# Block attention: the second head's scores are shifted inside ScalarE's exponential, the first head's stay with VectorE

## The chip, the cores and the metric

The kernel runs on one core of a Trainium2 chip. A core has five engines that work side by side and meet through semaphores: TensorE (PE in the rows; its weight loads are PEld), VectorE (DVE), ScalarE (ACT), GpSimd (POOL) and SyncE (SP), which issues transfers. The metric is device time in microseconds (us) of one execution, lower is better. A profiled execution gives the trace from which the rows below are taken.

## The reference

128 sequences of 128 tokens go through two layers of width 64. The change touches the first half of one block, a causal attention with 4 query heads and 2 key heads of width 16, whose core is:

```python
h = _rmsnorm(x, ln1_w)
q, k, v = ...                       # per head, q and k with rotary tables
scores = jnp.einsum('bhtd,bhsd->bhts', q, k) / jnp.sqrt(jnp.float32(HD))
scores = jnp.where(causal[None, None], scores, jnp.float32(-1e+30))
att = jax.nn.softmax(scores, axis=-1)
y = jnp.einsum('bhts,bhsd->bhtd', att, v).transpose(0, 2, 1, 3).reshape(Bx, Tx, Cx)
x = x + y @ wo.T
```

The softmax subtracts each row's maximum before the exponential. Everything before (embedding and a first attention) and after (experts, a decay attention, a selected MLP) is left as it was.

## The kernel before

The program is five phases, one after the other, with a barrier between them. The block attention (`phase_block_attention`) is the second. It holds 32 groups of 4 sequences (`GB` = 4; a sequence of 128 tokens is one block of 128 columns), and each group is done in two rounds K, since a round handles two of the four heads: `NQ` = 64 rounds. In round K, `m = K // 2` is the group and `j = K % 2` says which pair of heads. Here a round with j = 0 is called even, one with j = 1 odd. `e` = 0 is the first head of the pair and `e` = 1 the second.

One round goes like this. TensorE writes the scores of both heads to `bS` (`b_S` in the rows), two PSUM banks, one for each head, 512 columns each: two products that lay down the causal mask (L643), and eight small ones with the scores (L650). VectorE takes the maximum over each block of 128 columns (L924, 8 maxima for each row: 2 heads, 4 blocks), then subtracts it from both heads in one instruction that moves 1024 columns from PSUM to `pr` in SBUF (L930). ScalarE exponentiates `pr` in place in one instruction (L840). In the next round TensorE transposes `pr` head by head into `bT` (`turn`, L662), ScalarE copies each result out (`keep`, L785), and TensorE multiplies it with the values (L672).

There is one `bS`. So the scores of round K + 1 may be written once those of round K have been read, and `scores` waits for that on the semaphore `shifted`. There are two `pr`.

Each engine runs a list written out by hand for K = -7 to 72, in which the steps of several groups are interleaved (projections for later groups, output and routing of earlier ones), and each engine works its list strictly in order. On ScalarE the exponential of round K stands behind both `keep` of round K - 1, and in even rounds also behind `logits` (L807); behind it stand the small root computations of the layer norms (L847 to L857 in even rounds, L863 to L870 in odd ones). On VectorE the maximum and the shift stand next to each other in every round. GpSimd and SyncE take no part in the scores; GpSimd uses what ScalarE's small steps make (`b_rms` for `b_xn` at L603, `b_ss` for `moe_rows` at L615).

Of the kernel before, what the change touches and what calls it, by code (L numbers as in the profile page):

```python
# [6 lines left out]
ALU = mybir.AluOpType  # L7
ACT = mybir.ActivationFunctionType
# [5 lines left out]
P = 128  # L14
D = 64
GB = 4
# [50 lines left out]
def over(ap, width):  # L67

    return ap[:, :, None].to_broadcast([ap.shape[0], ap.shape[1], width])
# [415 lines left out]
def phase_block_attention(nc, dram, H, rows, logits, sent, ident, NB):  # L485
# [8 lines left out]
    with ExitStack() as ctx:  # L494
        m_ = Mem(nc, ctx)
# [19 lines left out]
        k1 = m_.sb("b_k1", [P, W])  # L515
        v = [m_.sb(f"b_v{u}", [P, GB, NKV, STRIP]) for u in range(2)]
        mx = [m_.sb(f"b_mx{u}", [P, 2, GB]) for u in range(2)]
        pr = [m_.sb(f"b_pr{u}", [P, 2, W]) for u in range(2)]
        pT = [m_.sb(f"b_pT{u}", [P, W]) for u in range(PT)]
        attT = m_.sb("b_attT", [P, W])  # L520
# [6 lines left out]
        bS = m_.ps("b_S", [P, 2, 512])  # L527
# [4 lines left out]
        kept = m_.sem("b_kept")  # L532

        U = {name: m_.sem(f"b_{name}") for name in
             ("scored", "max_made", "shifted", "exped", "turned", "pT_kept")}

        G = {name: m_.sem(f"bg_{name}") for name in
             ("summed", "mean_made", "centred", "squared", "spread", "log_var", "rstd_made", "x_made", "rstd_sq",
# [11 lines left out]
        def after(eng, name, n):  # L550

            if n >= 0:
                eng.wait_ge(G[name], min(n, NG - 1) + 1)

        def cols(b):
            return slice(b * P, (b + 1) * P)

        def place(b):

            return b % 2, slice(b // 2 * P, (b // 2 + 1) * P)  # L560
# [9 lines left out]
        with nc.Block() as block:  # L570
# [60 lines left out]
            def _(pe):  # L631
                pe.wait_ge(ready, READY)

                def scores(K):
                    m, j = K // 2, K % 2
                    s = m % 2
                    if j == 0:
                        pe.wait_ge(G["q_kept"], m + 1)
                        pe.wait_ge(G["k_made"], m + 1)
                    if K >= 1:  # L640
                        pe.wait_ge(U["shifted"], K)
                    for e in range(2):
                        nc.tensor.matmul(bS[:, e, :], ident_b[:], hide[:, None, :].to_broadcast([P, GB, P]),  # L643
                                         start=True, stop=False)
                    for b in range(GB):
                        half, c = place(b)
                        c = slice(half * HALF + c.start, half * HALF + c.stop)
                        for e in range(2):
                            r = slice(STRIP * (2 * j + e), STRIP * (2 * j + e + 1))
                            last = nc.tensor.matmul(bS[:, e, cols(b)], q[s][r, c], k0[s][r, c], start=False,  # L650
                                                    stop=(b == GB - 1))
                    last.then_inc(U["scored"], 1)

                def turn(K, e):
                    w = 2 * K + e
                    pe.wait_ge(U["exped"], K + 1)
                    if w >= 1:
                        pe.wait_ge(U["pT_kept"], w)
                    if K % 2 and e == 0:
                        after(pe, "y_made", K // 2 - 1)  # L660
                    for b in range(GB):
                        last = nc.tensor.transpose(bT[:, cols(b)], pr[K % 2][:, e, cols(b)], ident[:])  # L662
                    last.then_inc(U["turned"], 1)
# [112 lines left out]
            def _(act):  # L776
# [3 lines left out]
                def keep(K, e):  # L780
                    w = 2 * K + e
                    act.wait_ge(U["turned"], w + 1)
                    if w >= PT:
                        act.wait_ge(G["attended"], (w - PT) // NH + 1)
                    nc.scalar.activation(pT[w % PT][:], bT[:], ACT.Copy).then_inc(U["pT_kept"], 1)  # L785

                for K in range(FIRST, LAST + 1):
# [22 lines left out]
                    else:  # L810
# [25 lines left out]
                        if 0 <= K - 1 < NQ:  # L836
                            keep(K - 1, 1)
                    if 0 <= K < NQ:
                        act.wait_ge(U["shifted"], K + 1)
                        nc.scalar.activation(pr[K % 2][:], pr[K % 2][:], ACT.Exp).then_inc(U["exped"], 1)  # L840
                    if j == 0:
                        n = m + 3
                        if there(n):
# [29 lines left out]
            def _(dve):  # L873
# [21 lines left out]
                for K in range(FIRST, LAST + 1):  # L895
# [25 lines left out]
                    if 0 <= K < NQ:  # L921
                        u = K % 2
                        dve.wait_ge(U["scored"], K + 1)
                        nc.vector.tensor_reduce(mx[u][:].rearrange("p e b -> p (e b)"),  # L924
                                                bS[:].rearrange("p e (b t) -> p (e b) t", t=P), AX, ALU.max)\
                            .then_inc(U["max_made"], 1)
                        dve.wait_ge(U["max_made"], K + 1)
                        if K >= 2:
                            dve.wait_ge(U["turned"], 2 * (K - 1))
                        nc.vector.tensor_tensor(pr[u][:].rearrange("p e (b t) -> p (e b) t", t=P),  # L930
                                                bS[:].rearrange("p e (b t) -> p (e b) t", t=P),
                                                over(mx[u][:].rearrange("p e b -> p (e b)"), P), ALU.subtract)\
                            .then_inc(U["shifted"], 1)
                    if j == 0:
                        n = m + 3
                        if there(n):
# [1457 lines left out]
```

## Time and profile before

| | us |
|---|---|
| median of 3 runs | 2656.37 |
| the 3 runs | 2630.66, 2656.37, 2674.85 |
| the profiled execution | 2635.22 |
| its span, first to last instruction | 2633.4 |
| block attention: first scores to the last shift | 357.5 to 727.6 |
| maxima on VectorE in it (L924) | 64 of 1.22 each |
| shifts on VectorE in it (L930) | 64 of 1.22 each |
| exponentials on ScalarE in it (L840) | 64 of 1.05 each |

A row of the timeline says when an instruction (or a run of like ones) began, counted from the start of the span, how long it took, engine, line, operation, result and operands with their shapes; in brackets stands how long the engine had been idle and what ended that. The duration of a run of matmuls reaches to the modelled end of the last, so it overlaps the next row a little.

### The profile page before, as it was taken

The page shows a single profiled execution, that of the slowest core. Times are in us where ns is not written, and L with a number is a line of the kernel's source. Part 1 is how long each engine was busy: PE and PEld are TensorE (multiplying, and loading weights), DVE is VectorE, ACT ScalarE, POOL GpSimd, SP SyncE. Part 2 cuts the span into 40 slices and gives each one's busy share as a digit, 9 for nine tenths or more (in the row PEclk, how much of TensorE's full clock was granted, in tenths as well). Part 3 has the DMA queues.
Part 4 walks back from the last instruction along what each step waited for, and adds up shares of the span by engine and source line. Part 5 has one row for each costly group of instructions (what it writes and reads, how often), then busy time and mean ns, then how long its engine had stood idle before and what let it go on. Part 6 is the DMA issues. An engine that isn't in the chain of part 4 may idle for free. (4 is left out here: it accounts for less than half of the span.)

```text
span 2633.4 us, 56014 instructions
## 1 busy us (share of the span) xinstructions
PE 2170.0 (82%) x20636; PEld 1641.2 (62%) x20636; DVE 1790.5 (68%) x3688; ACT 1297.2 (49%) x2690; POOL 1733.5 (66%) x1900
## 2 busy tenths in 40 slices
PE   6999769999923699997289899889999998998495
PEld 5888647777723445444167677677777776776374
DVE  4899457777759644444377878878888788875524
ACT  1344136666621244443056666666666666664332
POOL 6565024444312577775499999999999999875361
PEclk9999579999955699999587888877778888875577
DMA  2111000000004255567100000000000000000003
GB/s 47 35 41 33 0 9 26 22 26 26 22 20 2 59 133 132 134 131 107 31 6 6 6 5 6 5 5 6 5 6 6 5 5 4 2 2 2 3 1 64
DMA packets 105741, 78.14 MB, mean 30 GB/s; under 512 B 71533, under 2 KB 92269, under 8 KB 105488
## 3 DMA queue, kind: packets, MB, share of 16 engines
q0 software_dynamic: 23344, 53.01, 9.5%
q1 hardware_dynamic: 82144, 21.74, 4.4%
q8 instruction: 161, 2.64, 0.4%
q14 instruction: 92, 0.75, 0.1%
HBM read 56.03 MB, written 18.68 MB: 28 GB/s over the span
## 5 line engine op out<-in xcount | busy, mean ns | idle before, releaser
L1906 DVE TENSOR_TENSOR_SCAN d_later<-d_cont,d_ex 128x768 f32<-128x768 f32 x128 | 279.2, 2182 | 30.8 <-ACT d_ex L1719 30.6
L1689 ACT ACTIVATE d_pT<-d_T 128x384 f32<-128x384 f32 x256 | 125.1, 489 | 291.9 <-PE d_T L1550 291.7
L1550 PE MATMUL d_T<-ident,d_p 128*128 128x128 f32 x768 | 170.7, 341 | 88.8 <-POOL d_p L1475 83.2
L1457 POOL TENSOR_TENSOR d_decay<-d_later,d_posg 128x768 f32<-128x768 f32 x128 | 233.0, 1820 | 7.7 <-DVE d_later L1906 7.7
L1461 POOL TENSOR_TENSOR d_decay<-d_decay,d_rtot 128x512 f32<-128x512 f32 x128 | 183.2, 1431 | 18.4
L1468 POOL DMA_INDIRECT d_moe<-back_rows,slot x128 | 137.6, 1075 | 73.3 <-DVE d_mean L1857 49.9
L1537 PEld LDWEIGHTS d_S<-d_kT,d_qT 16*128 16x128 f32 x2048 | 150.8, 221 | 51.2 <-issue 51.2
L1883 DVE SCALAR_TENSOR_TENSOR d_p<-d_decay,d_R 128x768 f32<-128x768 f32 x128 | 121.6, 950 | 87.5 <-PE d_R L1537 51.9
L1537 PEld LDWEIGHTS d_R<-d_kT,d_qT 16*128 16x128 f32 x2048 | 148.7, 218 | 51.3 <-issue 51.3
L1474 POOL TENSOR_TENSOR d_p<-d_p,d_mx 128x512 f32<-128x512 f32 x128 | 159.2, 1244 | 28.6 <-DVE d_mx L1889 26.8
L1537 PE MATMUL d_S<-d_kT,d_qT 16*128 16x128 f32 (+1 forms) x2048 | 170.0, 314 | 0.0
L1550 PEld LDWEIGHTS d_T<-ident,d_p 128*128 128x128 f32 x768 | 96.0, 165 | 116.9 <-POOL d_p L1475 93.5
L1537 PE MATMUL d_R<-d_kT,d_qT 16*128 16x128 f32 (+1 forms) x2048 | 167.8, 311 | 0.0
L1725 ACT ACTIVATE d_decay<-d_decay 128x768 f32<-128x768 f32 x128 | 107.3, 838 | 79.7 <-POOL d_decay L1462 79.5
L223 POOL DMA_INDIRECT rows<-in_table,idx x128 | 122.0, 953 | 35.6 <-issue 31.3
L1462 POOL TENSOR_TENSOR d_decay<-d_decay,d_rtot 128x256 f32<-128x256 f32 x128 | 140.3, 1096 | 0.0
L1327 DVE TENSOR_TENSOR e_cont<-e_h,e_upto 128x512 f32<-128x512 f32 x91 | 62.9, 691 | 104.7 <-ACT e_upto L1200 104.7
L1608 PE MATMUL d_X<-d_conv,d_xT 128*128 128x128 f32 x640 | 112.7, 354 | 1.5 <-ACT d_xT L1778 1.5
L1608 PEld LDWEIGHTS d_X<-d_conv,d_xT 128*128 128x128 f32 x640 | 111.2, 271 | 2.6 <-ACT d_xT L1778 2.6
L1719 ACT ACTIVATE d_ex<-d_ex 128x768 f32<-128x768 f32 x128 | 107.6, 840 | 7.9 <-DVE d_ex L1875 7.2
L594 POOL TENSOR_SCALAR b_mean<-b_mean 128x4 f32<-128x4 f32 x32 | 7.0, 220 | 156.4 <-DVE b_mean L965 156.3
L1727 ACT ACTIVATE d_decay<-d_decay 128x768 f32<-128x768 f32 x128 | 107.9, 843 | 4.1
(403 smaller groups left out, 6226.1 us busy)
## 6 DMA issues: line engine op xcount, KB each, us to landing
sent_rows<-moe_rows SPq DMA_DIRECT2D x32, 256.0 KB, 2.8
back_rows<-e_ys SPq DMA_DIRECT2D x91, 64.0 KB
out_h<-g_Y SPq DMA_DIRECT2D x8, 512.0 KB, 4.0
rows<-in_table,idx POOLq DMA_INDIRECT x128
d_moe<-back_rows,slot POOLq DMA_INDIRECT x128, 2.5
e_tie<-sent_rows,e_token POOLq DMA_INDIRECT x62
e_pick<-sent_rows,e_token POOLq DMA_INDIRECT x60
e_both<-sent_rows,e_token POOLq DMA_INDIRECT x60, 3.1
```

Of the source, the lines that this page charges most:

```text
L223: pool.indirect_dma_start(rows[u][:, b, :], None, dram["table"], bass.IndirectOffsetOnAxis(ap=idx[u][:, b:b + 1], axis=0))\
L1457: pool.tensor_tensor(decay[d][:], later[u][:, 0:2 * SEG].rearrange("p (e s) -> p e s", e=2), posg[:, h:h + 2, :], ALU.mult).then_inc(U["pl ...
L1461: pool.tensor_tensor(long(decay[d]), long(decay[d]), wide(rtot[u], 1, P), ALU.mult)
L1462: pool.tensor_tensor(short(decay[d]), short(decay[d]), wide(rtot[u], 0, HALF), ALU.mult)\
L1468: pool.indirect_dma_start(moe[n % KEEP_M][:, j, :], None, back_rows, bass.IndirectOffsetOnAxis(ap=slot[:, b:b + 1], axis=0))\
L1474: pool.tensor_tensor(long(p2[w]), long(p2[w]), wide(mx2[u], 1, P), ALU.subtract)
L1537: last = nc.tensor.matmul(bank[:, e, cols], qT[s][r, c, (2 * g + S) * P:(2 * g + S + 1) * P], kT[s][r, c, keys], start=False, stop=(g == 1 ...
L1550: last = nc.tensor.transpose(bT[:, t * P:(t + 1) * P], p2[K % KEEP_P][:, e, t * P:(t + 1) * P], ident[:])
L1608: last = nc.tensor.matmul(X1[:, g * P:(g + 1) * P], xT[:, g, tap:tap + P], conv[:, tap, :], start=(tap == 0), stop=(tap == TAPS - 1))
L1689: nc.scalar.activation(pT[w % KEEP_T][:], bT[:, 0:SEG], ACT.Exp).then_inc(U["pT_kept"], 1)
L1883: nc.vector.scalar_tensor_tensor(p2[w][:], decay[d][:], 1e-5, bR[:, :, 0:SEG], ALU.max, ALU.mult).then_inc(U["weighed"], 1)
L1906: nc.vector.tensor_tensor_scan(later[u][:, 1:1 + 2 * SEG], cont[:], ex[u][:].rearrange("p e s -> p (e s)"), 0.0, ALU.mult, ALU.add)\
```

## The change

The first head keeps its path: VectorE subtracts its maxima (512 columns now) and ScalarE exponentiates them in SBUF in one instruction. The second head no longer passes VectorE: VectorE makes the negative of its four maxima (`minus`, 128x4), and ScalarE reads its scores straight from PSUM, in four instructions of 128 columns, one for each block, with the block's column of `minus` as the bias of the exponential. ScalarE does the second head first. `exped` now counts these four for each round, and the first head has a semaphore of its own, `near_exped`. TensorE's `scores` waits for `exped` as well, since ScalarE now reads `bS`.

```diff
+        minus = [m_.sb(f"b_minus{u}", [P, GB]) for u in range(2)]
...
                     if K >= 1:
                         pe.wait_ge(U["shifted"], K)
+                        pe.wait_ge(U["exped"], GB * K)
...
                 def turn(K, e):
                     w = 2 * K + e
-                    pe.wait_ge(U["exped"], K + 1)
+                    if e == 0:
+                        pe.wait_ge(U["near_exped"], K + 1)
+                    else:
+                        pe.wait_ge(U["exped"], GB * (K + 1))
...
                     if 0 <= K < NQ:
+                        u = K % 2
+                        act.wait_ge(U["minus_made"], K + 1)
+                        if K >= 2:
+                            act.wait_ge(U["turned"], 2 * (K - 1))
+                        for b in range(GB):
+                            nc.scalar.activation(pr[u][:, 1, cols(b)], bS[:, 1, cols(b)], ACT.Exp, bias=minus[u][:, b:b + 1])\
+                                .then_inc(U["exped"], 1)
                         act.wait_ge(U["shifted"], K + 1)
-                        nc.scalar.activation(pr[K % 2][:], pr[K % 2][:], ACT.Exp).then_inc(U["exped"], 1)
+                        nc.scalar.activation(pr[u][:, 0, :], pr[u][:, 0, :], ACT.Exp).then_inc(U["near_exped"], 1)
...
-                        nc.vector.tensor_tensor(pr[u][:].rearrange("p e (b t) -> p (e b) t", t=P),
-                                                bS[:].rearrange("p e (b t) -> p (e b) t", t=P),
-                                                over(mx[u][:].rearrange("p e b -> p (e b)"), P), ALU.subtract)\
-                            .then_inc(U["shifted"], 1)
+                            dve.wait_ge(U["exped"], GB * (K - 1))
+                        nc.vector.tensor_scalar(minus[u][:], mx[u][:, 1, :], -1.0, None, ALU.mult).then_inc(U["minus_made"], 1)
+                        nc.vector.tensor_tensor(pr[u][:, 0, :].rearrange("p (b t) -> p b t", t=P),
+                                                bS[:, 0, :].rearrange("p (b t) -> p b t", t=P),
+                                                over(mx[u][:, 0, :], P), ALU.subtract).then_inc(U["shifted"], 1)
```

ScalarE's list at the end of an even round, and the start of the odd one, in the kernel before (in brackets the semaphores that an instruction waits for):

```order
L785 ACTIVATE b_pT<-b_T 128x512 [waits bg_attended,b_turned]
L807 ACTIVATE logits<-b_XB 128x2x2x8 [waits bg_routed]
L840 ACTIVATE b_pr<-b_pr 128x1024 [waits b_shifted]
L847 ACTIVATE b_rstd<-b_ss 128x4 [waits bg_msq_made,bg_x_made,bg_spread]
L850 ACTIVATE b_rstd<-b_rstd 128x4 [waits bg_log_var]
```

The same place in the changed kernel:

```order
L790 ACTIVATE b_pT<-b_T 128x512 [waits bg_attended,b_turned]
L812 ACTIVATE logits<-b_XB 128x2x2x8 [waits bg_routed]
L849 ACTIVATE b_pr<-b_S,b_minus 128x128 [waits b_turned,b_minus_made]
L849 ACTIVATE b_pr<-b_S,b_minus 128x128 x3
L852 ACTIVATE b_pr<-b_pr 128x512 [waits b_shifted]
L859 ACTIVATE b_rstd<-b_ss 128x4 [waits bg_msq_made,bg_x_made,bg_spread]
```

One instruction on `pr` has become five, and the first four read `bS`; their place behind the copy and the logits is the same.

TensorE's list from the projections of an even round to the scores of the odd one, in the kernel before:

```order
L680 MATMUL b_XA<-b_xT,f_wk 128x256 [waits bg_v_kept,bg_x2_made,bg_xT_kept]
L680 MATMUL b_XB<-b_xT,f_wkp 128x256 [waits bg_logits_kept,bg_yT_kept,bg_q_kept]
L643 MATMUL b_S<-hide,ident_b 128x512 [waits b_shifted]
L643 MATMUL b_S<-hide,ident_b 128x512
L650 MATMUL b_S<-b_k,b_q 128x128 x8
```

The same place in the changed kernel:

```order
L685 MATMUL b_XA<-b_xT,f_wk 128x256 [waits bg_v_kept,bg_x2_made,bg_xT_kept]
L685 MATMUL b_XB<-b_xT,f_wkp 128x256 [waits bg_logits_kept,bg_yT_kept,bg_q_kept]
L645 MATMUL b_S<-hide,ident_b 128x512 [waits b_exped,b_shifted]
L645 MATMUL b_S<-hide,ident_b 128x512
L652 MATMUL b_S<-b_k,b_q 128x128 x8
```

Nothing moved on TensorE; the first product of the scores waits for ScalarE's four instructions as well.

## Rows read from the trace of the kernel before

**Rows 1.** Busy time (count) of the engines by stretch, granted clock, DMA share, GB/s

```profile
400.00:500.00 100.00, 94.96 (x1112) 72.05 (x1108) 75.84 (x130) 66.87 (x171) 42.65 (x68) 1.00 0.08 23
...
720.00:730.00 10.00, 8.37 (x108) 6.32 (x104) 6.16 (x9) 6.36 (x13) 1.91 (x3) 1.00 0.09 28
```

**Rows 2.** Timeline of TensorE, from the scores of one even round to the next

```profile
507.32 0.59 PE L643 MATMUL b_S<-hide,ident_b 128*128 128x512 bf16 x2
...
508.93 0.66 PE L662 MATMUL b_T<-ident,b_pr 128*128 128x128 f32 x4
...
510.37 0.63 PE L662 MATMUL b_T<-ident,b_pr 128*128 128x128 f32 x4 [0.56 <-ACT b_pT L785]
...
511.93 0.70 PE L680 MATMUL b_XB<-b_xT,f_wkp 64*128 64x256 f32 x4
512.56 0.61 PE L643 MATMUL b_S<-hide,ident_b 128*128 128x512 bf16 x2
...
515.91 0.60 PE L747 MATMUL b_XB<-ident,moe_rows 128*128 128x128 f32 x4
...
519.11 0.59 PE L643 MATMUL b_S<-hide,ident_b 128*128 128x512 bf16 x2
```

**Rows 3.** Timeline of ScalarE, the same stretch

```profile
505.91 0.60 ACT L785 ACTIVATE b_pT<-b_T 128x512 f32<-128x512 f32 x1 [0.30 <-PE b_T L662]
506.40 1.05 ACT L840 ACTIVATE b_pr<-b_pr 128x1024 f32<-128x1024 f32 x1
...
507.94 0.20 ACT L870 ACTIVATE b_rms<-b_rms 128x4 f32<-128x4 f32 x1
...
509.63 0.60 ACT L785 ACTIVATE b_pT<-b_T 128x512 f32<-128x512 f32 x1 [0.21 <-PE b_T L662]
...
511.03 0.60 ACT L785 ACTIVATE b_pT<-b_T 128x512 f32<-128x512 f32 x1 [0.54 <-PE b_T L662]
511.59 0.20 ACT L807 ACTIVATE logits<-b_XB 128x32 f32<-128x32 f32 x1
511.68 1.05 ACT L840 ACTIVATE b_pr<-b_pr 128x1024 f32<-128x1024 f32 x1
```

**Rows 4.** Timeline of VectorE, the same stretch

```profile
507.28 0.15 DVE L957 TENSOR_TENSOR b_rsq<-b_rstd 128x4 f32<-128x4 f32 x1
...
510.35 1.22 DVE L930 TENSOR_TENSOR b_pr<-b_S,b_mx 128x1024 f32<-128x1024 f32 x1
```

**Rows 5.** ScalarE instructions by line and shape: busy us, mean ns, idle before

```profile
L1689 ACT ACTIVATE d_pT<-d_T 128x384 f32<-128x384 f32 x256 | 125.1, 489 | 291.9 <-PE d_T L1550 291.7
...
L1189 ACT ACTIVATE e_xT<-e_X,e_ln 128x256 f32<-128x256 f32 x91 | 43.1, 473 | 46.6 <-PE e_X L1119 46.3
L2141 ACT ACTIVATE g_hid<-g_H,g_b 128x512 f32<-128x512 f32 x64 | 40.5, 683 | 33.3 <-PE g_H L2067 33.3
...
L820 ACT ACTIVATE b_xT<-b_XA 128x256 f32<-128x256 f32 x32 | 12.1, 379 | 2.2 <-PE b_XA L694 2.1
...
L832 ACT ACTIVATE b_v<-b_XA 128x128 f32<-128x128 f32 x32 | 8.9, 277 | 1.7 <-PE b_XA L688 1.6
```

**Rows 6.** Timeline of ScalarE in the last phase, two like instructions together

```profile
2499.80 1.26 ACT L2141 ACTIVATE g_hid<-g_H,g_b 128x512 f32<-128x512 f32 x2 [1.64 <-PE g_H L2067]
```

**Rows 7.** Timeline of ScalarE and TensorE at the start of rounds 2 and 63

```profile
368.03 1.05 ACT L840 ACTIVATE b_pr<-b_pr 128x1024 f32<-128x1024 f32 x1
...
368.06 0.61 PE L643 MATMUL b_S<-hide,ident_b 128*128 128x512 bf16 x2
...
723.40 0.60 PE L643 MATMUL b_S<-hide,ident_b 128*128 128x512 bf16 x2
723.49 1.05 ACT L840 ACTIVATE b_pr<-b_pr 128x1024 f32<-128x1024 f32 x1
```

**Rows 8.** Timeline of GpSimd, the same stretch as in groups 2 to 4

```profile
508.92 0.61 POOL L603 TENSOR_TENSOR b_xn<-b_x,b_rms 128x256 f32<-128x256 f32 x1
...
513.47 1.19 POOL L615 TENSOR_TENSOR moe_rows<-b_x,b_ss 128x256 f32<-128x256 f32 x2 [3.25 <-ACT b_ss L857]
```

More of the change, by code:

```diff
@@ L534, in phase_block_attention @@
         U = {name: m_.sem(f"b_{name}") for name in
-             ("scored", "max_made", "shifted", "exped", "turned", "pT_kept")}
+             ("scored", "max_made", "minus_made", "shifted", "near_exped", "exped", "turned", "pT_kept")}
         G = {name: m_.sem(f"bg_{name}") for name in
```

## The prediction

> **What bounds the kernel now.** I began with the busy time by stretch. In the stretch from 400 to 500 us, in the middle of the block attention, TensorE is busy 94.96 of 100 us at a granted clock of 1.00 (its upper level, 2.4 GHz), VectorE 75.84 and ScalarE 66.87 [rows 1]. The clock stands there through the steady part of the phase. Busy shares don't say which wait ends last, so the timeline of one group came next. TensorE starts the scores of an even round at 507.32 and those of the next even round at 519.11 [rows 2], so a group of two rounds takes 11.79 us. Within it TensorE's runs touch each other (the projection that begins at 511.93 and takes 0.70 reaches past 512.56, where the scores begin), apart from one gap of 0.56 us at 510.37, where it waits for ScalarE's copy of the first transposed head [rows 2]. So the phase is one chain along TensorE's list, and whatever holds its next instruction back by some tenths lengthens the round by as much.
>
> What matters is therefore the moment at which the scores of the next round may be written. In the even round VectorE's shift begins at 510.35 and takes 1.22, so `bS` is free at 511.57 [rows 4], while TensorE comes to the scores only at 512.56 [rows 2]: 0.99 us to spare. VectorE is not on the chain. In that place ScalarE now reads `bS` too, and ScalarE's exponential begins late: at 511.68 in the even round, since it stands behind the copy at 511.03 (which waited for TensorE's transposition) and the logits at 511.59; in the odd round at 506.40, behind the copy at 505.91 [rows 3]. From there to TensorE's next scores there are 0.88 us (512.56 - 511.68) and 0.92 us (507.32 - 506.40) [rows 2, 3]. If the four reads and the signal to TensorE fit in this, the change costs nothing; if not, the rest is paid in every round.
>
> **The change part by part.** *One read of the second head.* A copy of 128x128 from PSUM takes 277 ns (L832). The function makes no difference that shows: the exponential of 384 columns from PSUM takes 489 ns (L1689), which is 110 ns over the copy of 256 columns (L820, 379), about what 128 more columns cost among copies (379 - 277 = 102) [rows 5]. A bias in an operand for each row costs extra: L1189 is the same copy of 256 columns with such an operand (as scale) and takes 473 instead of 379, so 94 ns [rows 5]. Together 277 + 94 = 371 ns.
>
> *Four of them.* Neighbours overlap: two of L2141, which have such a bias, take 1.26 us together where one takes 683 ns [rows 5, 6], so 2 x 0.683 - 1.26 = 0.11 us are shared. I take 0.10, so that four take 3 x 0.27 + 0.37 = 1.18 us. If nothing were shared it would be 4 x 0.37 = 1.48. The lower bound is 0.69: one copy of 512 columns (0.60, the copy at 505.91 [rows 3]) with 0.094 for the operand. The value lies near the middle; I take it since rows 6 is the same form of instruction on the same engine, side by side.
>
> *The signal.* The copy that starts at 509.63 ends at 510.23 [rows 3], and the transposition that waits for it begins at 510.37 [rows 2]: 0.14 us from ScalarE's end to TensorE's start.
>
> *The new wait.* 1.18 + 0.14 = 1.32 us are needed. In an even round 0.88 are there, so TensorE is held up by 0.44 us; in an odd round by 1.32 - 0.92 = 0.40 us. Behind the held instruction stand all of TensorE's list and, through it, every other engine. The delay is not caught up within the group: the next round's transpositions, the copies behind them and so the next four reads are all timed by TensorE's own start of the scores. A group becomes 11.79 + 0.84 = 12.63 us. The other conditions of the reads are met long before: the maxima are there at 510.35, before the shift starts [rows 4].
>
> *Sum over the phase.* There are 63 starts of scores that wait for a round before. In 54 of them, from round 8 to round 61, the room is 0.88 to 0.92 as in the group above: 54 x 0.42 = 22.7 us. In the other nine TensorE has less work between, because some of the interleaved steps are not there yet or are over. The scores of round 2 begin 0.03 us after the exponential of round 1, so they are held up by 1.29; those of round 63 begin 0.09 before that of round 62, so by 1.41 [rows 7]. By the same subtraction all nine make 7.3 us; in the first of them, where ScalarE stands idle, the reads can start behind the maxima, and 0.21 us are lost. Together 30.0 us.
>
> *What goes from VectorE.* The shift of 1.22 us halves its columns, and `minus` comes, a 128x4 instruction of about 0.15 (L957) [rows 4]. I take this at nothing, since VectorE had 0.99 us to spare where it meets TensorE. Should that cover be gone it would be worth under 1.22 / 2 - 0.15 = 0.46 us a round, as a gain.
>
> *What ScalarE does later.* The first head's exponential has half of 1024 columns, an estimate of 0.61 us from 1.05 for 1024 [rows 3] and 0.28 for 128 [rows 5]. The four reads and it keep ScalarE for 4 x 0.27 + 0.61 = 1.69 instead of 1.05, so what stands behind is 0.6 us later. Three readers could notice. The transposition of the first head at 508.93 [rows 2]: it moves to 509.33 with the scores, and the exponential is done at 506.40 + 1.69 = 508.09. `b_xn` on GpSimd at 508.92 [rows 8], which needs `b_rms`, finished at 508.14 [rows 3] and then at 508.8. `moe_rows`, from 513.47 to 514.66 [rows 8], for the transposition at 515.91 [rows 2]: 1.25 us of room for 0.6. All three hide it; without that cover it would be at most 0.6 us a group, 19 us. SyncE's transfers follow `moe_rows` and nothing waits for them in the phase.
>
> So the profiled execution's 2635.2 us become 2665.2. It lies 21 us below the median of the three runs; the same 30 us on the median 2656.4 give **2686.4 us**, 1.1% more.
>
> The Trainium skill's page "ScalarE: Activation LUTs", section "What ACT_TABLE_LOAD costs", prices an instruction with a bias in a pointer at 280 ns plus 0.833 ns a column, 387 ns here, with an overlap of 93 ns between neighbours. By that the four would take 3 x 0.294 + 0.387 = 1.27 us, an estimate, and the sum would be 63 x 0.09 = 5.7 us more, 2692. The rows of this kernel decide for me, since the copy from PSUM is measured here at 277. The same page's section "Rules for kernel authors" would have additions stay on VectorE; in this trace VectorE's addition lies beside TensorE's work and ScalarE's reading does not, so row and rule both point to a loss.
>
> **The rivals.** *The reads fit.* With the lower bound of 0.69 the need is 0.83 us, less than the room of 0.88 and 0.92, and only the nine odd starts cost anything, some 3 us: 2659. For it speaks that 0.44 us is a small difference of large terms; against it that this shape needs the sharing to be nearly whole, and rows 6 shows 0.11 of 0.68.
>
> *Nothing is shared.* With 1.48 us each of the 63 starts loses 0.30 more, 19 us: 2705. Against it stands the pair in rows 6; for it that the four write the same tile and bump the same semaphore, which the pair in rows 6 does as well.
>
> *VectorE was the bound.* If TensorE's scores waited for the shift, the change would give back up to 0.46 x 64 = 29 us, less whatever ScalarE adds: 2627 at best. Against it stands the 0.99 us to spare in rows 4 and 2.
>
> *Slower by much: the clock.* The new gaps lower TensorE's busy share from 0.95 to some 11.2 of 12.63 us, 0.89. If the granted clock fell to its lower level (1.2 GHz) for part of the phase, a group's 11.2 us of TensorE work would at most double: up to 11 us a group. The place would be the first rounds, where the starts lose up to 1.3 us each. It decides, that is passes 2% (53 us), once three of the 32 groups run so (30 + 33); with five it is 2686 + 55 = 2741. Against it: from 720 to 730 us TensorE was busy 8.37 of 10 us and kept a clock of 1.00 [rows 1].
>
> *The change not doing what it says* I exclude: the lists of both kernels show the instructions and waits in place.
>
> **How the numbers follow.** Forecast 0.75; reads fit 0.08; nothing shared 0.07; the clock 0.07; VectorE the bound 0.03. About 2%, 53 us, is what a measurement of this kernel tells from no change; its three runs alone lie 44 us apart (22 about the middle). The range takes in both bounds of the reads (2659 and 2705), and some 7 us outside on either side for the scatter of a median: 2652 to 2712. It leaves out the clock, the gain, and little of the rest. Faster by over 2%: 0.02, where the best case of a gain meets the scatter. Slower by over 2%: the clock's 0.07 and about 0.05 from the upper half of "nothing shared" and the forecast's scatter, 0.12. Within 2%: 0.86.
>
> **What would show it.** Four reads of about 0.37 us, starting 0.27 apart; TensorE's first product of the scores with an idle time of about 0.4 us before it that ScalarE ends, in nearly every round; 12.6 us from one even round's scores to the next; the phase some 30 us longer, the other phases alike. Later phases that differ by tens of us, a granted clock under 1.00 between 400 and 700 us, or reads that end before TensorE comes, would make it wrong.

## The result, and the profile after

Before: 2657.2 us, median of 4 runs (2630.66 to 2674.85). After: 2682.39 us, median of 4 (2651.76 to 2719.68). The two medians lie 25.2 us apart. The ratio is 1.0163 with a 95% interval of 1.0097 to 1.0228: slower, by 1 to 2.3%. It leaves out executions that are over 1.5% longer than the fastest of their kernel, while the medians take in all. The forecast was 2686.4.

The profiled execution took 2651.76 us. Its span of 2650.0 is 16.6 us longer than that of before. That is less than the block attention lost, as the parts show (first and last start of the scores on TensorE bound the block attention):

| us | before | after | difference |
|---|---|---|---|
| start to the first scores | 357.5 | 354.6 | -2.9 |
| first to last scores | 365.9 | 397.9 | +32.0 |
| the rest | 1910.0 | 1897.5 | -12.5 |
| of it the last phase, first to last `g_hid` on ScalarE (L2141 before, L2154 after) | 129.1 | 119.4 | -9.7 |

The kernel after, busy time by stretch (columns as in [rows 1]):

```profile
400.00:500.00 100.00, 90.85 (x1054) 67.43 (x1050) 67.65 (x137) 71.74 (x224) 40.56 (x64) 1.00 0.08 23
```

TensorE fell from 94.96 to 90.85, VectorE from 75.84 to 67.65, ScalarE rose from 66.87 to 71.74 [rows 1]. No engine became full. All did less in 100 us, apart from ScalarE: something waits that did not. The list of TensorE's waits between 355 and 760 us names it (total, times, longest):

```profile
PE b_S L645 <- ACT b_pr L849: 20.1, 62, 1.4
```

62 of the 63 starts of scores that follow a round now wait for ScalarE's reads. One group of two rounds on TensorE (508.53 and 521.07 are the scores of even rounds, 514.17 those of the odd round between them):

```profile
508.53 0.59 PE L645 MATMUL b_S<-hide,ident_b 128*128 128x512 bf16 x2 [0.20 <-ACT b_pr L849]
...
510.14 0.66 PE L667 MATMUL b_T<-ident,b_pr 128*128 128x128 f32 x4
...
513.14 0.70 PE L685 MATMUL b_XB<-b_xT,f_wkp 64*128 64x256 f32 x4
514.17 0.59 PE L645 MATMUL b_S<-hide,ident_b 128*128 128x512 bf16 x2 [0.33 <-ACT b_pr L849]
...
517.50 0.60 PE L752 MATMUL b_XB<-ident,moe_rows 128*128 128x128 f32 x4
...
521.07 0.59 PE L645 MATMUL b_S<-hide,ident_b 128*128 128x512 bf16 x2 [0.20 <-ACT b_pr L849]
```

And ScalarE in the same group:

```profile
506.75 0.60 ACT L790 ACTIVATE b_pT<-b_T 128x512 f32<-128x512 f32 x1 [0.30 <-PE b_T L667]
507.25 1.14 ACT L849 ACTIVATE b_pr<-b_S,b_minus 128x128 f32<-128x128 f32 x4
508.25 0.66 ACT L852 ACTIVATE b_pr<-b_pr 128x512 f32<-128x512 f32 x1
...
512.79 0.20 ACT L812 ACTIVATE logits<-b_XB 128x32 f32<-128x32 f32 x1
512.89 1.14 ACT L849 ACTIVATE b_pr<-b_S,b_minus 128x128 f32<-128x128 f32 x4
513.89 0.66 ACT L852 ACTIVATE b_pr<-b_pr 128x512 f32<-128x512 f32 x1
```

From one even round's scores to the next (508.53 to 521.07) a group takes 12.54 us, where it took 11.79 [rows 2]. From the first read to the scores there are 1.28 us in both rounds: 507.25 to 508.53 and 512.89 to 514.17. That is four reads (1.14) and the signal (0.14). There were 0.88 and 0.92 [rows 2, 3], so the scores start 0.40 and 0.36 us late, 0.76 a group, which is the 0.75 by which the group grew. The projection ahead shows the same: it begins 1.03 us before the scores (513.14 to 514.17), where it began 0.63 before [rows 2]. (The idle time in brackets, 0.33 and 0.20, is smaller: it counts from the modelled end of the last product.)

### The profile page after: what moved, and what is told of

Same layout as the page of the kernel before. It is cut to its first block and busy times, and to the rows that moved or that the text cites. A ratio compares the mean times of both kernels' runs of the same rounds, so it can differ in the third digit from the quotient of the medians.

```text
span 2650.0 us, 56459 instructions
## 1 busy us (share of the span) xinstructions
PE 2180.1 (82%) x20636; PEld 1645.3 (62%) x20636; DVE 1774.4 (67%) x3752; ACT 1334.5 (50%) x2946; POOL 1727.9 (65%) x1900
## 5 line engine op out<-in xcount | busy, mean ns | idle before, releaser
L1487 POOL TENSOR_TENSOR d_p<-d_p,d_mx 128x512 f32<-128x512 f32 x128 | 165.6, 1294 | 28.6 <-DVE d_mx L1902 26.8
L1474 POOL TENSOR_TENSOR d_decay<-d_decay,d_rtot 128x512 f32<-128x512 f32 x128 | 169.9, 1327 | 18.4
L1481 POOL DMA_INDIRECT d_moe<-back_rows,slot x128 | 128.1, 1001 | 75.1 <-DVE d_mean L1870 51.7
L1475 POOL TENSOR_TENSOR d_decay<-d_decay,d_rtot 128x256 f32<-128x256 f32 x128 | 153.5, 1199 | 0.0
L1738 ACT ACTIVATE d_decay<-d_decay 128x768 f32<-128x768 f32 x128 | 107.3, 838 | 73.2 <-POOL d_decay L1475 73.2
L616 POOL TENSOR_TENSOR moe_rows<-b_x,b_ss 128x256 f32<-128x256 f32 x64 | 37.9, 614 | 132.8 <-ACT b_ss L869 132.8
L1621 PE MATMUL d_X<-d_conv,d_xT 128*128 128x128 f32 x640 | 120.8, 372 | 1.5 <-ACT d_xT L1791 1.5
L1621 PEld LDWEIGHTS d_X<-d_conv,d_xT 128*128 128x128 f32 x640 | 120.1, 290 | 2.6 <-ACT d_xT L1791 2.6
L936 DVE TENSOR_REDUCE b_mx<-b_S 128x8 f32<-128x1024 f32 x64 | 78.4, 1225 | 58.4 <-PE b_S L652 58.2
```

The lines of the kernel that those rows point to most:

```text
L1474: pool.tensor_tensor(long(decay[d]), long(decay[d]), wide(rtot[u], 1, P), ALU.mult)
L1475: pool.tensor_tensor(short(decay[d]), short(decay[d]), wide(rtot[u], 0, HALF), ALU.mult)\
L1481: pool.indirect_dma_start(moe[n % KEEP_M][:, j, :], None, back_rows, bass.IndirectOffsetOnAxis(ap=slot[:, b:b + 1], axis=0))\
L1487: pool.tensor_tensor(long(p2[w]), long(p2[w]), wide(mx2[u], 1, P), ALU.subtract)
L1621: last = nc.tensor.matmul(X1[:, g * P:(g + 1) * P], xT[:, g, tap:tap + P], conv[:, tap, :], start=(tap == 0), stop=(tap == TAPS - 1))
```

## The experiments

The theory (T): ScalarE's four reads of `bS` stand at the end of its list for the round, behind the copies, and TensorE's next scores wait for the last of them. Against it: ScalarE's greater load alone delays what follows (R1); VectorE's new order and waits (R2); or the gaps made the clock rise later (R3), since the scores of after ran at 0.50 for longer. Each kernel was traced; the measure is the period of a group, which does not depend on how long the other phases took in that execution.

| kernel | period of a group, us | first to last scores, us | full clock, us after the first scores |
|---|---|---|---|
| before | 11.79 | 365.9 | 6.6 |
| before, second trace | 11.79 | 372.3 | 22 |
| after | 12.54 | 397.9 | 22 |
| after, second trace | 12.54 | 397.5 | 22 |
| one read in place of four | 11.79 | 374.6 | 23 |
| four reads without the operand | 11.84 | 376.7 | 23 |
| before, with the wait alone | 12.36 | 395.9 | 29 |
| before, with ScalarE's load alone | 11.79 | 369.7 | 15 |
| reads ahead of the second copy | 12.16 | 384.5 | 22 |
| before, scores earlier in TensorE's list | 11.49 | 366.9 | 26 |
| both orders, one read | 11.37 | 361.2 | 22 |

**One read.** In the kernel after, one exponential of 512 columns takes the place of the four, with the maximum of the first block:

```diff
-                        for b in range(GB):
-                            nc.scalar.activation(pr[u][:, 1, cols(b)], bS[:, 1, cols(b)], ACT.Exp, bias=minus[u][:, b:b + 1])\
-                                .then_inc(U["exped"], 1)
+                        nc.scalar.activation(pr[u][:, 1, :], bS[:, 1, :], ACT.Exp, bias=minus[u][:, 0:1])\
+                            .then_inc(U["exped"], GB)
```

> The changed kernel, but ScalarE reads the second head in one instruction of 512 columns with the first block's column as bias, so three blocks are shifted by the wrong maximum. The measure is the time from the first to the last start of scores on TensorE (365.9 us before, 398.2 us changed) and the period of a group in the steady part (11.79 and 12.54). If the loss is the time that the reads take in front of TensorE's scores: one read is about 0.69 us, with 0.14 for the signal 0.83, less than the room of 0.88 and 0.92, so the period is 11.79 again and the stretch 367 to 374. Rival, the loss comes with VectorE's new order or the extra waits, whatever the reads take: the period stays at 12.4 to 12.6 and the stretch near 395.

ScalarE's timeline in that kernel, an even round's read:

```profile
510.03 0.68 ACT L848 ACTIVATE b_pr<-b_S,b_minus 128x512 f32<-128x512 f32 x1
```

TensorE's timeline, from even to even round:

```profile
505.66 0.59 PE L645 MATMUL b_S<-hide,ident_b 128*128 128x512 bf16 x2
...
510.91 0.60 PE L645 MATMUL b_S<-hide,ident_b 128*128 128x512 bf16 x2
...
517.46 0.59 PE L645 MATMUL b_S<-hide,ident_b 128*128 128x512 bf16 x2
```

0.68 + 0.14 = 0.82 us fit into the 0.88 between 510.03 and 510.91: no idle time, and the period of before. The wait, VectorE's new order and the split of the exponential are all still in this kernel; only the length of the reading changed. That is against R2, and the rival "the reads fit" is what this kernel shows, with a shape that the change doesn't have. The stretch of 374.6 us misses what was expected by a little: that range was built on the trace of before in which the clock rose after 6.6 us; with 22 us, as here, before itself takes 372.3.

**Four reads without the operand.** The bias is left out and a fixed factor stands in its place:

```diff
-                            nc.scalar.activation(pr[u][:, 1, cols(b)], bS[:, 1, cols(b)], ACT.Exp, bias=minus[u][:, b:b + 1])\
+                            nc.scalar.activation(pr[u][:, 1, cols(b)], bS[:, 1, cols(b)], ACT.Exp, scale=2.0 ** -6)\
```

> The changed kernel with its four reads, but without the bias column: the second head is exponentiated with a fixed scale and no maximum, so its weights are not the softmax's. If the 94 ns of the operand for each row is what tips it: four reads take 3 x 0.175 + 0.28 = 0.80 us, with the signal 0.94, so the even rounds lose 0.06 and the odd ones 0.02, a period of 11.87 and a stretch of 368 to 376. Rival, it is the number of instructions and not the operand: the period stays above 12.3 and the stretch above 388.

ScalarE's timeline in that kernel, an even round's reads:

```profile
509.14 0.78 ACT L849 ACTIVATE b_pr<-b_S 128x128 f32<-128x128 f32 x4
```

TensorE's timeline, two even rounds:

```profile
504.77 0.59 PE L645 MATMUL b_S<-hide,ident_b 128*128 128x512 bf16 x2
...
516.61 0.59 PE L645 MATMUL b_S<-hide,ident_b 128*128 128x512 bf16 x2
```

The four take 0.78 in place of 1.14: the operand costs 0.36 us, nearly all of the 0.36 to 0.40 that a round lost. 0.78 + 0.14 = 0.92, against 0.88 and 0.92 of room, is just too much behind the even round's reads, and the period is 11.84, 0.05 over before. With this the length of the reads alone, in one instruction or four, has taken the period through 11.79, 11.84 and 12.54.

**The wait alone.** Before, and TensorE waits for its old exponential of 1024 columns as well:

```diff
                         pe.wait_ge(U["shifted"], K)
+                        pe.wait_ge(U["exped"], K)
```

> The kernel before with one wait added: the scores wait for the whole exponential of the round before, which doesn't read the scores. All results are as before. If a late ScalarE in front of the scores is what costs: 1.05 + 0.14 = 1.19 us are needed where 0.88 and 0.92 are there, so 0.31 and 0.27 are lost, the period is 12.37 and the stretch 384 to 392. Rival, the loss comes from ScalarE's extra work or from the new shape of the instructions: with neither here, the period stays at 11.79 and the stretch at 366.

ScalarE's timeline in that kernel, the even round:

```profile
510.91 1.05 ACT L841 ACTIVATE b_pr<-b_pr 128x1024 f32<-128x1024 f32 x1
```

TensorE's timeline, even, odd and even round:

```profile
506.55 0.59 PE L644 MATMUL b_S<-hide,ident_b 128*128 128x512 bf16 x2
...
512.10 0.59 PE L644 MATMUL b_S<-hide,ident_b 128*128 128x512 bf16 x2 [0.24 <-ACT b_pr L841]
...
518.91 0.59 PE L644 MATMUL b_S<-hide,ident_b 128*128 128x512 bf16 x2
```

510.91 + 1.05 + 0.14 = 512.10, to the hundredth. The need is 1.19 against 0.88 and 0.92, so 0.58 a group by the prediction's subtraction, and 12.36 - 11.79 = 0.57 was measured. One added wait, with no work moved at all, brings most of the loss.

**The load alone.** Before, with ScalarE's four short exponentials and the one of 512 columns, but all reading what VectorE has shifted:

```diff
+                        act.wait_ge(U["shifted"], K + 1)
+                        for b in range(GB):
+                            nc.scalar.activation(pr[u][:, 1, cols(b)], pr[u][:, 1, cols(b)], ACT.Exp, bias=minus[u][:, b:b + 1])\
+                                .then_inc(U["exped"], 1)
...
-                        nc.scalar.activation(pr[K % 2][:], pr[K % 2][:], ACT.Exp).then_inc(U["exped"], 1)
+                        nc.scalar.activation(pr[u][:, 0, :], pr[u][:, 0, :], ACT.Exp).then_inc(U["near_exped"], 1)
```

> ScalarE's new load without the wait: VectorE shifts both heads as in the kernel before (and makes the small column, of zeros), ScalarE does the second head in four instructions of 128 columns with a bias column, but from SBUF, and the first head in one; the scores wait for VectorE's shift alone. Results as before. If the read in front of the scores is what costs: the period is 11.79 and the stretch 366 to 369. Rival, ScalarE's longer list is what costs: about 0.8 us of extra work in a round lengthen the period to 12.3 or more and the stretch to 382 or more.

ScalarE's timeline in that kernel, the short exponentials of an odd and an even round:

```profile
507.90 1.26 ACT L847 ACTIVATE b_pr<-b_pr,b_minus 128x128 f32<-128x128 f32 x4
...
513.24 1.29 ACT L847 ACTIVATE b_pr<-b_pr,b_minus 128x128 f32<-128x128 f32 x4
```

TensorE's timeline, two even rounds:

```profile
508.82 0.59 PE L644 MATMUL b_S<-hide,ident_b 128*128 128x512 bf16 x2
...
520.62 0.59 PE L644 MATMUL b_S<-hide,ident_b 128*128 128x512 bf16 x2
```

These two starts lie 11.80 apart, and the mean of the groups is 11.79: the period stays, although ScalarE's exponentials take no less than in the kernel after. R1 falls: the instructions cost nothing until TensorE's scores wait for them.

**The reads ahead of the second copy.** In the kernel after, in even rounds, the four reads move ahead of the second copy of `b_T` and of the logits (`far` holds the reads, `near` the first head's exponential):

```diff
-                        if 0 <= K - 1 < NQ:
-                            keep(K - 1, 1)
+                        if 0 <= K < NQ:
+                            far(K)
...
+                        if 0 <= K - 1 < NQ:
+                            keep(K - 1, 1)
```

> The changed kernel with ScalarE's list in even rounds in another order: the four reads straight after the copy of y, then the logits, then the second copy of the transposed head (in odd rounds as in the changed kernel). All results as before. If the place of the reads behind the copies is what costs: in even rounds the reads can start 3.2 us after the start of the scores, are done at 4.4 and free the scores at 4.5, before TensorE comes at 5.24, so the even rounds lose nothing, the odd ones still 0.36: a period of 12.15 us (12.54 changed) and a stretch of 383 to 390. Rival, the reads' bare work costs wherever it stands, because the copies and the logits behind it come later: the period stays at 12.4 or more, the stretch near 396.

ScalarE's timeline in that kernel, the even round:

```profile
512.01 1.14 ACT L798 ACTIVATE b_pr<-b_S,b_minus 128x128 f32<-128x128 f32 x4
```

TensorE's timeline, even, odd and even round:

```profile
508.81 0.59 PE L645 MATMUL b_S<-hide,ident_b 128*128 128x512 bf16 x2 [0.20 <-ACT b_pr L798]
...
514.06 0.60 PE L645 MATMUL b_S<-hide,ident_b 128*128 128x512 bf16 x2
...
520.97 0.59 PE L645 MATMUL b_S<-hide,ident_b 128*128 128x512 bf16 x2 [0.20 <-ACT b_pr L798]
```

The scores behind the even round's reads (514.06) no longer wait. Those behind the odd round's reads, which were left as they were, wait for the same 0.20 as in the kernel after. The period is 12.16, so 0.38 of the 0.75 are gone. So the loss belongs to the place of the reads in ScalarE's list, and to each round by itself.

**The same kernels again.** Two traces more, of before and of after, unchanged, for R3.

> The kernel before once more, for the moment at which TensorE's granted clock reaches its upper level in this phase: 6.6 us after the first scores in the first trace of it, 22.4 in the changed kernel's, 15 to 29 in four others. If the added waits of the first rounds put the rise off, it comes within 8 us here. Rival, it differs from execution to execution: later here.

> The changed kernel once more. Both theories of the loss expect the period of 12.54 us. On the clock: if the added waits put the rise off, it comes 20 us or more after the first scores again; if it differs from execution to execution, anywhere from 6 to 29.

The second traces, busy time in stretches of 2 us (the granted clock is the last column but two). Before:

```profile
376.00:378.00 2.00, 2.00 (x10) 0.52 (x8) 1.38 (x2) 0.83 (x3) 0.09 (x1) 0.54 0.00 0
378.00:380.00 2.00, 2.00 (x49) 1.68 (x49) 0.94 (x1) 0.00 (x0) 1.75 (x2) 1.00 0.00 0
```

After, second trace:

```profile
394.00:396.00 2.00, 2.00 (x9) 1.18 (x10) 0.69 (x1) 1.98 (x6) 0.00 (x0) 0.51 0.00 0
396.00:398.00 2.00, 2.00 (x34) 1.46 (x38) 1.02 (x2) 0.46 (x3) 1.06 (x1) 1.00 0.00 0
```

The same view of the first trace of before shows the rise earlier:

```profile
362.00:364.00 2.00, 1.42 (x6) 0.13 (x2) 2.00 (x4) 0.87 (x1) 0.00 (x0) 0.50 0.00 0
364.00:366.00 2.00, 2.00 (x23) 1.61 (x22) 1.29 (x3) 0.80 (x4) 1.24 (x2) 0.96 0.00 0
```

The first scores of these three began at 355.7, 373.9 and 357.5 us, so the rise came 22, 22 and 6.6 us later. The clock rises from its lower level (1.2 GHz) to its upper (2.4) late in before as well, without the change. The early rise was seen in one of two traces of before and in none of three of after, so whether the change makes it rarer stays open; but the period is taken where the granted clock is 1.00 in both kernels, and R3 falls as the cause of the longer period. The early rise is worth 372.3 - 365.9 = 6.4 us. Between the two second traces, with a like rise, the change costs 397.5 - 372.3 = 25.2 us; of the 32.0 of the first two, 6.4 were the clock's. Five of the stretches that were expected came out longer than their ranges, which lean on the trace with the early rise: 374.6 us for at most 374 with one read, 376.7 for 376 without the operand, 395.9 for 392 with the wait alone, 369.7 for 369 with the load alone, and 366.9 for 356 with the order that follows.

**Other orders.** Can the room be made instead of the reading shortened? In the kernel before, the first of the two projections moves into the gap of 0.56 us ahead of the second transposition [rows 2], and an odd round's scores move from the top of that round to behind the router, ahead of the second projection:

```diff
+                        if there(m + 1):
+                            pe.wait_ge(G["xT_kept"], m + 2)
+                            after(pe, "x2_made", m - 3)
+                            after(pe, "v_kept", m)
+                            project(XA, wk, m + 1, "k0_made")
                         if 0 <= K - 1 < NQ:
                             turn(K - 1, 1)
...
+                        if 0 <= K < NQ:
+                            scores(K + 1)
```

> The kernel before, with TensorE's list in even rounds in another order: the first key projection goes into the 0.56 us gap before the second transposition, and the scores of the odd round go ahead of the second key projection. If TensorE's list is the chain and VectorE has 0.99 us to spare: the scores of the odd round start when VectorE's shift ends, 4.30 us after those of the even round instead of 5.24, and 0.54 comes back behind them, so the period is 11.4 instead of 11.79 and the stretch 352 to 356. Rival, the keys of the next group now come too late for VectorE and GpSimd, whose lists hold it: 11.7 or more, the stretch at 364 or more.

TensorE's timeline in that kernel, with the first projection at 507.24:

```profile
504.82 0.59 PE L643 MATMUL b_S<-hide,ident_b 128*128 128x512 bf16 x2
...
507.24 0.70 PE L680 MATMUL b_XA<-b_xT,f_wk 64*128 64x256 f32 x4
507.87 0.66 PE L662 MATMUL b_T<-ident,b_pr 128*128 128x128 f32 x4
...
509.13 0.60 PE L643 MATMUL b_S<-hide,ident_b 128*128 128x512 bf16 x2
...
516.31 0.59 PE L643 MATMUL b_S<-hide,ident_b 128*128 128x512 bf16 x2
```

The gap of 0.56 is filled, and the period falls to 11.49, not to the 11.4 expected: the odd round's scores start 4.31 us after the even round's, as forecast, but from there to the next even round's it now takes 7.18 us, where it took 6.55 [rows 2]. The stretch of 366.9 us lies where the rival had it (364 or more), with a clock that rose only after 26 us; the period lies below the rival's 11.7. The ratio to before was 0.9899 (0.9798 to 1.0000), one end at no change, so it was timed again:

> The kernel before with TensorE's other order (e6), more executions. The period of 11.49 instead of 11.79 is worth 32 x 0.30 = 10 us less: a ratio of 0.996. If a shorter phase is given back in later phases: 1.000.

0.9974 (0.9934 to 1.0015): no gain that this measurement tells from nothing.

Then this order with the change in it, the reads early as in the fifth kernel and made one, with one negated maximum for the four blocks of a row:

```diff
-                    for b in range(GB):
-                        nc.scalar.activation(pr[u][:, 1, cols(b)], bS[:, 1, cols(b)], ACT.Exp, bias=minus[u][:, b:b + 1])\
-                            .then_inc(U["exped"], 1)
+                    nc.scalar.activation(pr[u][:, 1, :], bS[:, 1, :], ACT.Exp, bias=minus[u][:, 0:1])\
+                        .then_inc(U["exped"], GB)
...
-                        nc.vector.tensor_scalar(minus[u][:], mx[u][:, 1, :], -1.0, None, ALU.mult).then_inc(U["minus_made"], 1)
+                        nc.vector.tensor_reduce(minus[u][:, 0:1], mx[u][:, 1, :], AX, ALU.max, negate=True).then_inc(U["minus_made"], 1)
```

> TensorE's order of e6 with the change in another form: VectorE makes one negative maximum of the second head's four blocks for each row (the softmax doesn't depend on which number is subtracted, as long as the exponentials stay in range), ScalarE reads that head in one instruction of 512 columns, in even rounds straight after the copy of y. If the time at which the scores are read sets the next scores: in even rounds VectorE's half shift is done about 3.8 us after the start of the scores and the read about 4.0, so TensorE starts the next scores when its own list comes to them, at 4.1 instead of 4.3, and in odd rounds 0.68 + 0.14 fits in the 0.92 there: a period of 11.25 to 11.35 us (11.49 in e6, 11.79 before), 14 to 17 us less over the phase than before at equal clocks. Rival, ScalarE's later copies or the later keys hold TensorE back: 11.49 or more.

1.0014 (0.9974 to 1.0054). One of its 12 executions took 4556.17 us and is not in the ratio; the cause is not known. In a second comparison:

> The kernel of e7, more executions. The period of 11.37 is worth 32 x 0.42 = 13 us less: a ratio of 0.995. The first comparison said 1.0014 with an interval of 0.9974 to 1.0054; if a shorter phase is given back in later phases, it stays at 1.000 or above.

0.9898 (0.9847 to 0.9948). The two intervals don't overlap, although the kernel is the same; the medians of all executions of the second, 2638.35 and 2653.82 us, give 0.9942. TensorE's timeline in the second, even, odd and even round:

```profile
509.52 0.59 PE L645 MATMUL b_S<-hide,ident_b 128*128 128x512 bf16 x2
...
513.70 0.60 PE L645 MATMUL b_S<-hide,ident_b 128*128 128x512 bf16 x2
...
520.89 0.59 PE L645 MATMUL b_S<-hide,ident_b 128*128 128x512 bf16 x2
```

The period is 11.37 in both traces, and the block attention takes 361.2 and 359.0 us, 5 to 13 less than in the two traces of before. With a like rise of the clock (22 us) it is 372.3 - 361.2 = 11.1 us, where 14 to 17 and a period of 11.25 to 11.35 were expected. So the phase gains, and whether the whole does stays open: 0.5% is less than these comparisons agree to.

**After, timed once more**, beside the last two:

> The changed kernel against the one before, more executions on one chip, beside e6 and e7. The traces put the loss of the phase at 25 us at equal clocks of its first rounds: a ratio of 1.0095. A theory in which the loss is the 43 us that the first comparison's middle says would give 1.016.

2696.89 us (6 runs) against 2653.82: 1.0178 (1.0124 to 1.0232), more than the 1.0095 that the trace's 25 us give. Its block attention took 397.5 us with the period of 12.54, like the other two traces of after.

## Why the prediction held, point by point

**The mechanism** was the one forecast: the room of 0.88 and 0.92 us, four reads and a signal that do not fit, a hold-up in every round that is not caught up within the group. Five kernels move the period by changing the length of the reads, the wait or the place, and each lands within 0.03 us of the period that was expected from the subtraction. The two kernels with TensorE's other order missed it, by 0.09 and by 0.02 us.

**The four reads** took 1.14 us, forecast 1.18. One read takes 371 ns, as forecast; the reads' line in the kernel after:

```profile
L849 ACT ACTIVATE b_pr<-b_S,b_minus x256: 359/371/388, 359.2 to 761.2; 128x128 f32<-128x128 f32 x128
```

(min, median, max, first and last start.) So (1.14 - 0.371) / 3 = 0.256 lies between starts, and neighbours share 0.115 where I took 0.10. That is the mis-sized term: 0.04 a round. An estimate from the figures of the Trainium skill's page "ScalarE: Activation LUTs", section "What ACT_TABLE_LOAD costs", is 1.27. The four from PSUM do not agree with it, and the measurement decides; the same four read from SBUF, in the load-alone kernel, took 1.26 and 1.29, which do.

**The signal** was 0.14, as forecast: in the wait-alone kernel 510.91 + 1.05 = 511.96, and TensorE begins at 512.10.

**The sum.** A group lost 0.75 for the 0.84 forecast, so 54 starts cost 27 x 0.75 = 20.2 us, forecast 22.7. The nine others cost 25.2 - 20.2 = 5.0, forecast 7.3; the longest idle time before the scores was 1.4 us, where the prediction had 1.41 for round 63. Start by start, the two second traces show where the rest is missing: the first three starts lost 0.87 together, and the subtraction had 0.21 + 1.29 + 0.89 = 2.39. In both traces they ran at the clock's lower level, while the prediction took their room from a trace in which the upper level was there from round 2 on. The sum has no term for that. Together 25.2 against 30.0, at a like rise of the clock.

**The medians and the ratios.** The two medians of the result lie 25.2 us apart, just what the traces show. That the 2682.4 also lies near 2686.4 is in part luck, since the four executions of before spread over 44 us and those of after over 68. The middles of the two ratios are 43 and 47 us, the intervals begin at 26 and 33, and the traces show 25 to 32. The surplus doesn't come from the phases between the block attention and the last: the span without the first phase, the block attention and the last phase took 1781 and 1776 us in the traces of before, and 1778 in each of the three of after. What scatters is the first phase, 347 to 387 us, and the last, 119 to 151, and the code of both is the same in all kernels. The activation of the last phase by its line (columns as in the reads' line above), before:

```profile
L2141 ACT ACTIVATE g_hid<-g_H,g_b x64: 679/684/687, 2473.0 to 2602.1; 128x512 f32<-128x512 f32 x64
```

and before with the wait alone:

```profile
L2142 ACT ACTIVATE g_hid<-g_H,g_b x64: 679/684/689, 2495.5 to 2646.2; 128x512 f32<-128x512 f32 x64
```

Every instruction takes the same 684 ns, and the phase 129.1 and 150.7 us. Busy time and granted clock of the two stretches (columns as in [rows 1]):

```profile
2473.00:2602.10 129.10, 124.40 (x796) 100.95 (x797) 30.21 (x94) 51.18 (x93) 54.97 (x84) 0.79 0.00 1
2495.50:2646.20 150.70, 149.00 (x797) 120.39 (x797) 29.84 (x94) 51.32 (x94) 55.03 (x84) 0.65 0.00 1
```

The same work took longer where TensorE's granted clock was lower, and so it is in all fourteen traces: about 119 us at 0.88, 129 at 0.79, 134 at 0.78, 145 at 0.71 and 151 at 0.65. In the three traces of after this phase took 119, 119 and 129 us, in the two of before 129 and 119: these five show no tie to the change. The longest first phase, 387 us, is that of the third trace of after, and before with TensorE's other order took as long there in its second trace. Scatter of that size can cover the 15 to 20 us; that it does so in the executions that were not traced was not shown, and stays open. The prediction had named later phases that differ by tens of us as a sign against it: they do differ so, from execution to execution, but with no tie to the change in these traces.

**What was costed at nothing.** VectorE was off the chain, as forecast: its shift of the first head in the kernel after begins at 511.60, takes 0.68 and ends 1.89 us before the scores at 514.17. The transposition of the first head (510.14) and that of `moe_rows` (517.50) begin without idle time. `moe_rows` itself did move by the 0.6 us forecast. It began 6.15 us after the scores of the even round [rows 2, 8], and now 6.75 after the even round's 508.53, on GpSimd's timeline:

```profile
515.28 1.18 POOL L616 TENSOR_TENSOR moe_rows<-b_x,b_ss 128x256 f32<-128x256 f32 x2 [4.21 <-ACT b_ss L869]
```

Its room of 1.25 covers this.

**The rivals.** "The reads fit" fails for four reads and is true of one (11.79). "Nothing is shared" fails at 0.115 shared. "VectorE was the bound" fails: the wait-alone kernel leaves VectorE as it was and loses 0.57 a group, and the change gives nothing back. "The clock" fails in the steady part, where the granted clock was 1.00 in every hundred us from 400 to 700. In the first rounds, the place that this rival named, it was at its lower level for 22 us, but so it was in the second trace of before.

## What to carry to other kernels

Before work moves from one engine to another, ask who gives a shared PSUM bank back last: the price is not the busy time but the time from the new reader's start, late in its own list, to the moment at which the writer wants the bank. Here 0.36 us for a bias operand on four short instructions turned room into a wait; one read of all columns took the wait away, and the reads further ahead in ScalarE's list did so in the rounds in which they were moved. When phases scatter by more than the effect, measure the period in the trace, not the total.

## What the runs showed of the hardware that was not expected

**A tiny VectorE instruction that takes two to seven times as long in every other round.** `minus` (128x4, SBUF to SBUF) on VectorE's timeline in the kernel after:

```profile
504.62 0.56 DVE L943 TENSOR_SCALAR b_minus<-b_mx 128x4 f32<-128x4 f32 x1
...
511.52 0.17 DVE L943 TENSOR_SCALAR b_minus<-b_mx 128x4 f32<-128x4 f32 x1
511.60 0.68 DVE L944 TENSOR_TENSOR b_pr<-b_S,b_mx 128x512 f32<-128x512 f32 x1
```

GpSimd's timeline beside it:

```profile
503.88 1.27 POOL L623 TENSOR_TENSOR b_k<-b_k 128x512 f32<-128x512 f32 x1
```

The long one ends at 505.18, and GpSimd's sum at 505.15; in the other round GpSimd does nothing there. In the load-alone kernel the two, VectorE's and GpSimd's, begin nearly together:

```profile
505.27 1.15 DVE L941 TENSOR_SCALAR b_minus<-b_mx 128x4 f32<-128x4 f32 x1
505.13 1.27 POOL L623 TENSOR_TENSOR b_k<-b_k 128x512 f32<-128x512 f32 x1
```

Here `minus` takes 1.15 us and ends at 506.42, the sum at 506.40. With one read (0.50), without the operand (0.55) and with the early reads (0.40) it ends within 0.03 us of the sum as well. In the kernel with both orders a reduction to 128x1 stands in its place and takes 0.16 us in the midst of the same sum. It looks as if VectorE waited for GpSimd's instruction, and as if it depended on the form of its own; why, no experiment here tested. It was not on the chain: with 1.15 us the period is still 11.79.

**Four short reads took less from PSUM than from SBUF.** Four exponentials of 128 columns with a bias operand took 1.14 us from PSUM and 1.26 to 1.29 from SBUF. In the latter kernel they also write where they read, so the source alone was not taken apart.

**The clock's rise** came between 6.6 and 29 us after the first scores (29 in the wait-alone kernel), with the same code ahead of it, and between two traces of the same kernel that was worth 6.4 us.
